# A three-layer graph network on one core: layers one and two multiplied in pairs of states by Strassen's scheme

## What is computed

```
x = layernorm(x + L0(x, src, dst))          # three layers, this is where the change is
x = layernorm(x + L1(x, src, dst, ...))     # one message-passing block, untouched
def L0(x, Ws_self, Ws_neigh, bs, src, dst):
    deg = segment_sum(ones, dst)
    inv_deg = 1 / clip(deg, 1)
    h = x                                   # 3125 x 512
    for l in range(3):
        neigh = segment_sum(h[src], dst) * inv_deg
        h = h @ Ws_self[l] + neigh @ Ws_neigh[l] + bs[l]
        if l != 2: h = relu(h)
    return h
```

## Time and profile before

| | us |
|---|---|
| median of 3 runs (lowest, highest) | 1944.8 (1929.04, 1958.04) |
| span of the profiled execution | 1942.4 |
| TensorE busy in it | 1847.2 (95%) |
| VectorE busy in it | 1175.3 (61%) |
| ScalarE, GpSimd busy in it | 623.7 (32%), 1137.9 (59%) |

### The profile page before, as it was taken

How to read it: one execution, slowest core, us unless ns; L and a number is a source line. 1 busy time by engine, 2 the same in 40 slices (tenths; PEclk the granted TensorE clock), 3 DMA queues, 4 the chain that set the end, 5 groups by cost and what they waited for, 6 DMA issues and landing times.

```text
span 1942.4 us, 23120 instructions
## 1 busy us (share of the span) xinstructions
PE 1847.2 (95%) x7910; PEld 1133.5 (58%) x7910; DVE 1175.3 (61%) x1955; ACT 623.7 (32%) x1432; POOL 1137.9 (59%) x1087
## 2 busy tenths in 40 slices
PE   8999999999999989999999999999997699999987
PEld 4455555554555545555555556666665477777765
DVE  6866778677444433444344436555535489899977
ACT  1566532332000000000000000111115478788875
POOL 4400000364888877888788822777776667677770
PEclk9999999999999989999999999999998799999998
DMA  5365665433555344544444443566644234344340
GB/s 163 123 210 174 222 206 180 128 102 95 142 145 139 105 128 116 145 124 132 108 132 124 121 130 128 197 210 198 209 157 117 71 96 114 105 109 114 110 109 26
DMA packets 239540, 265.35 MB, mean 137 GB/s; under 512 B 130757, under 2 KB 176527, under 8 KB 239420
## 3 DMA queue, kind: packets, MB, share of 16 engines
q1 hardware_dynamic: 204028, 205.79, 34.7%
q0 software_dynamic: 34480, 57.58, 10.9%
q10 hardware_dynamic: 912, 0.46, 0.1%
HBM read 174.44 MB, written 89.27 MB: 136 GB/s over the span
## 4 chain that ended last, share of the span: by engine, by line
PE 70%; DVE 11%; issue 6%; ACT 4%; another core or an unknown queue 3%; POOL 3%; DMA 2%; SPq 0%; DVEq 0%; POOLq 0%; ACTq 0%
PE low L1228 37%; PE mid L1054 23%; PE low L1258 3%; PE top L1085 2%; DVE table L2023 1%; PE mid L1239 1%; ACT table L1491 1%; DVE sort L1831 1%; PE mid L1069 1%; DVE table L2026 1%; POOL sort L900 1%; POOL table L922 1%; DVE table L2040 1%; DVE wbuf L2002 1%
## 5 line engine op out<-in xcount | busy, mean ns | idle before, releaser
L1228 PE MATMUL low<-table,abuf 125*125 125x512 f16 x3750 | 844.0, 382 | 7.3 <-issue 7.2
L1228 PEld LDWEIGHTS low<-table,abuf 125*125 125x125 bf16 x3750 | 508.3, 137 | 315.2 <-issue 43.4
L1054 PE MATMUL mid<-wbuf,h_t 128*125 128x512 f32 x1200 | 556.5, 601 | 5.8 <-DVE st_out L1759 5.1
L917 POOL DMA_INDIRECT by_src<-scat_row,sort x416 | 487.1, 1171 | 126.1 <-issue 120.8
L922 POOL DMA_INDIRECT table<-msg_table,wbuf x270 | 294.3, 1090 | 128.3 <-issue 85.2
L1054 PEld LDWEIGHTS mid<-wbuf,h_t 128*125 128x125 f32 x1200 | 215.4, 189 | 217.3 <-issue 202.5
L1769 DVE SCALAR_TENSOR_TENSOR y<-low,inv_deg,st_in 125x512 f32<-125x512 f32 x75 | 56.1, 749 | 462.1 <-PE low L1228 309.7
L1713 DVE TENSOR_TENSOR abuf<-abuf,row_scale 125x750 bf16<-125x750 bf16 (+6 forms) x156 | 265.9, 1719 | 0.8
L949 POOL DMA_INDIRECT sort<-msg_table,sort x180 | 193.2, 1073 | 92.2 <-issue 54.5
L1258 PE MATMUL low<-table,wbuf 128*125 128x256 f32 x900 | 212.7, 387 | 18.1 <-ACT table L1491 11.2
L900 POOL TENSOR_TENSOR sort<-sort 128x416 f32<-128x416 f32 x26 | 31.9, 1226 | 320.7 <-DVE sort L1831 320.7
(11 more groups left out here) (245 smaller groups left out, 1595.8 us busy)
## 6 DMA issues: line engine op xcount, KB each, us to landing
abuf<-adj SPq DMA_DIRECT2D x75, 781.2 KB
adj<-table SPq DMA_DIRECT2D x25, 781.2 KB, 4.6
states<-st_out SPq DMA_DIRECT2D x75, 256.0 KB
st_in<-states SPq DMA_DIRECT2D x75, 256.0 KB
flips<-y_flip SPq DMA_DIRECT2D x48, 256.0 KB
h_t<-flips SPq DMA_DIRECT2D x192, 64.0 KB
early_rows<-sort POOLq DMA_DIRECT2D x35, 320.0 KB
table<-early_rows SPq DMA_DIRECT2D x24, 448.0 KB
```

The source lines that it names most:

```text
L917: pool.indirect_dma_start(out=by_src, out_offset=bass.IndirectOffsetOnAxis(ap=place_i[:, k * PIECE + j:k * PIECE + j + 1], axis=0), in_=sc ...
L1054: last = pe.matmul(to[0:TN, :], h_t[i % 2][:, k, 0:TN], weights[l % 2][:, a, k, :], start=k == 0, stop=k == KC - 1)
L1228: last = pe.matmul(p_agg[k % 2][0:TN, :], a_tile[k % 3][:, a, :], table[ps % 2][0:TN, a, h, :], start=a == 0 and h == 0, stop=a == TILES - ...
```

## The change

In each of the layers one and two, 22 of the 25 states are taken in pairs (r, q = r + 1). With the columns of a state cut in two halves of 256 and each weight matrix cut likewise, the two states' rows and own parts are four sums of eight *half products* (a half product is two f32 matmuls); the changed kernel forms them from seven half products with Strassen's sums of states and of weights. A pair takes 14 f32 matmuls in place of 16. Both states of a pair are multiplied in one aggregate (k % 25 = 3, 5, ... 23; r = k + 22), and the aggregate before or after it holds none. The states 22, 23 and 24 of a layer stay as they were.

- TensorE: `pair_first(r)` at a = 4 (four half products, in `p_pair`, which are the four banks of `mid`), `pair_second(r)` at a = 16 (three). In `pair_first` the second half product waits for `s_mixed`, that is for VectorE's `mix_states`; `pair_second` waits for `s_own` of r, that is for `unmix_first`.
- VectorE: `mix_states(r)`, four f32 instructions on 128 x 250, right behind `flip` in the pair's step; `unmix_first` (four on 125 x 512) behind the edge sort's first part; then `unmix_rows`, `row_scales` and `row_lo` of r and of q, `unmix_second`, all before the edge sort's second part. Two `own_part` go. `mix_weights` (four instructions on 128 x 1024) runs once a layer, at k = 1 and k = 26.
- ScalarE: `copy_first(r)` copies one PSUM bank to `st_out`; in k under 7 it stands between the first and the second block eviction. Both `row_hi` stand behind the last eviction.
- SyncE: `h_t` has four buffers in place of two; the weights of layer two are loaded at k = 25 in place of k = 2, because the mixed weights of a layer lie where the other layer's are.
- Some tiles of the sort share memory with other things; the masks of the bins wait for `bin_starts` in place of the counts.

```diff
     for a in range(TILES):                              # TensorE, aggregate k
-        for state in made_at(k):
+        for r in pair_begun(k):
+            if a == 4:
+                pair_first(r)
+        for r in pair_ended(k):
+            if a == 16:
+                pair_second(r)
+        for state in singles_at(k):
...
+    def pair_first(r):
+        for i in (r, q):
+            pe.wait_ge(s_fld[flips_to(i) % 2], flips_loaded(flips_to(i)))
+        pe.wait_ge(s_wmix, 1 + l)
+        pe.wait_ge(s_row, r)
+        pe.wait_ge(s_own, r)
+        pair_product(p_pair[0], h_t[q % HT][:, 0:HALF, :], upper).then_inc(s_half, 1)
+        pe.wait_ge(s_mixed, 1 + n + 1)
+        pair_product(p_pair[1], mixed[:, 1, :, :], wm[:, 0, HALF:KC, :]).then_inc(s_half, 1)
+        pair_product(p_pair[2], mixed[:, 0, :, :], wm[:, 0, 0:HALF, :]).then_inc(s_half, 1)
+        pair_product(p_pair[3], h_t[r % HT][:, 0:HALF, :], wm[:, 1, 0:HALF, :]).then_inc(s_ps, 1)
+    def pair_second(r):
+        pe.wait_ge(s_own, r + 1)
+        pair_product(p_pair[3], h_t[r % HT][:, HALF:KC, :], wm[:, 1, HALF:KC, :], False).then_inc(s_pn, 1)
+        pair_product(p_pair[0], h_t[q % HT][:, HALF:KC, :], w[:, 0, HALF:KC, :], False).then_inc(s_pn, 1)
+        pair_product(p_pair[2], mixed[:, 2, :, :], w[:, 1, HALF:KC, :], False).then_inc(s_ps, 1)
...
+    def mix_states(r):                                  # VectorE
+        for i in (r, q):
+            dve.wait_ge(s_fld[flips_to(i) % 2], flips_loaded(flips_to(i)))
+        ch.link(dve.tensor_tensor(s1, upper_r, lower_r, ALU.add))
+        dve.tensor_tensor(upper_r, upper_q, upper_r, ALU.subtract)
+        ch.link(dve.tensor_tensor(s2, s1, upper_q, ALU.subtract))
+        dve.tensor_tensor(s4, lower_q, s2, ALU.subtract).then_inc(s_mixed, 1)
...
         if k and by_dma(i):
             flip(i)
+        for one in pair_begun(k):
+            mix_states(one)
...
         place_bins(bins_first(k))
         if k == 13:
             places_last()
-        for state in made_at(k):
+        for one in pair_begun(k):
+            unmix_first(one)
+        for one in pair_ended(k):
+            unmix_rows(one)
+            for i in (one, one + 1):
+                row_scales(i)
+                row_lo(i)
+            unmix_second(one + 1)
+        if k in (1, TILES + 1):
+            mix_weights(k // TILES + 1)
+        for state in singles_at(k):
```

More of the change, by code:

```diff
@@ L144, in gnn_kernel @@
     y_flip = sb("y_flip", [P, D])
-    h_t = [sb(f"h_t{b}", [P, KC, P]) for b in range(2)]
+    h_t = [sb(f"h_t{b}", [P, KC, P]) for b in range(HT)]
+    mixed = sb("mixed", [P, 3, KC // 2, TN])
+    deg_row = mixed[0:TILES, 0, 0, :]
     row_max = sb("row_max", [P, 1])
@@ L312, in gnn_kernel @@
     p_s = p_mid[:, 3 * D:4 * D]
+    p_pair = [p_mid[:, b * D:(b + 1) * D] for b in range(4)]
     p_b = [p_top[:, 0:D], p_top[:, D:2 * D]]
@@ L517, in made_at, with paired, pair_begun, pair_ended @@
         return [n for n in (i - 1,) if by_dma(n)] + [n for n in (i,) if TILES <= n < AGGS and not by_dma(n)]
+    def paired(i):
+        return TILES <= i < AGGS and i % TILES < PAIRED
+    def pair_begun(k):
+        r = k + PAIRED
+        return [r] if k < 2 * TILES and 3 <= k % TILES <= PAIRED + 1 and k % TILES % 2 else []
+    def pair_ended(k):
+        return pair_begun(k)
+    def pair_ended_last(k):
+        return bool(pair_ended(k)) and first_tile(k + 1)
+    def pair_number(r):
+        l, t = divmod(r, TILES)
+        return (l - 1) * (PAIRED // 2) + t // 2
+    def rows_bank(i):
+        if paired(i):
+            return p_pair[3] if i % TILES % 2 == 0 else p_pair[0]
+        return p_n[i % 2]
+    def singles_at(k):
+        return [i for i in made_at(k) if not paired(i)]
+    def stored_at(k):
+        return pair_begun(k) + [r + 1 for r in pair_ended(k)] + singles_at(k)
     def flips_loaded(n):
@@ L782, in _ @@
                 if not first_tile(k):
-                    for i in made_at(k):
+                    for i in stored_at(k):
                         store_state(i)
@@ L1053, in product @@
                         pe.wait_ge(s_w0[k], 16)
-                    last = pe.matmul(to[0:TN, :], h_t[i % 2][:, k, 0:TN], weights[l % 2][:, a, k, :], start=k == 0, stop=k == KC - 1)
+                    last = pe.matmul(to[0:TN, :], h_t[i % HT][:, k, 0:TN], weights[l % 2][:, a, k, :], start=k == 0, stop=k == KC - 1)
                     if k == KC - 1:
@@ L1058, in product, with pair_product @@
                         between(a * KC + k)
+            def pair_product(to, rows, cols, first=True):
+                for c in range(HALF):
+                    last = pe.matmul(to[0:TN, :], rows[:, c, 0:TN], cols[:, c, :], start=first and c == 0, stop=c == HALF - 1, skip_group_check=True)
+                return last
+            def pair_first(r):
+                q, l, n = r + 1, r // TILES, pair_number(r)
+                upper = weights[l % 2][:, 0, 0:HALF, :]
+                for i in (r, q):
[5 more added lines that the diff above has]
+                pe.wait_ge(s_mixed, 1 + n + 1)
+                wm = weights[(l + 1) % 2]
+                pair_product(p_pair[1], mixed[:, 1, :, :], wm[:, 0, HALF:KC, :]).then_inc(s_half, 1)
+                pair_product(p_pair[2], mixed[:, 0, :, :], wm[:, 0, 0:HALF, :]).then_inc(s_half, 1)
+                pair_product(p_pair[3], h_t[r % HT][:, 0:HALF, :], wm[:, 1, 0:HALF, :]).then_inc(s_ps, 1)
+            def pair_second(r):
+                q, l = r + 1, r // TILES
+                w, wm = weights[l % 2], weights[(l + 1) % 2]
+                pe.wait_ge(s_own, r + 1)
+                pair_product(p_pair[3], h_t[r % HT][:, HALF:KC, :], wm[:, 1, HALF:KC, :], False).then_inc(s_pn, 1)
+                pair_product(p_pair[0], h_t[q % HT][:, HALF:KC, :], w[:, 0, HALF:KC, :], False).then_inc(s_pn, 1)
+                pair_product(p_pair[2], mixed[:, 2, :, :], w[:, 1, HALF:KC, :], False).then_inc(s_ps, 1)
             def message_product(i):
@@ L1068, in message_product @@
                 for k in range(4):
-                    last = pe.matmul(p_n[i % 2][0:TN, k * F:(k + 1) * F], h_t[i % 2][:, k, 0:TN], w_in_sb[:, min(k, 1), :], start=True, stop=True)
+                    last = pe.matmul(p_n[i % 2][0:TN, k * F:(k + 1) * F], h_t[i % HT][:, k, 0:TN], w_in_sb[:, min(k, 1), :], start=True, stop=True)
                 last.then_inc(s_pn, 1)
@@ L1939, in _ @@
                     one_hot_rows(builder_of(TILES + k + 1))
-                if k + 1 < AGGS:
+                if k + 1 < AGGS and not pair_ended_last(k):
                     scale(k + 1, 0)
```

101 lines of the change are left out of this document (75 added, 26 removed).

## The result

The changed kernel takes 2056.3 us (median of 4 runs, 2030.4 to 2067.8) against 1946.4 (4 runs): ratio 1.054, 95% interval 1.045 to 1.064. It is slower by 110 us where +60 was forecast, and lies above the range.

A forecast was written before the change was run, and what follows sets the result against it. TensorE, busy 95%, was taken to bound the kernel, with VectorE as full in aggregates 1 to 13. 71.4 us lost there less 11 gained later gave +60, about 2004 us (+3%), range 1968 to 2034.

The forecast's parts named there:

- the early stage: Aggregates 1 to 13, with six pairs: VectorE's backlog makes TensorE wait for mixing; loss of 71.4 us.
- Walk: Step-by-step timing of aggregates 1 to 13: aggregate 13 ends at 550.3, where it ended at 478.9 before.
- chain: From aggregate 7 on, VectorE and TensorE wait in turn: two steps take 49.5 us, against 37.1 for VectorE now.
- Prices: VectorE's added instructions: mixing about 1.70 us, `mix_weights` 4.9, adds 0.70 each; in all +4.5 us a pair.
- the other sixteen pairs: Pairs at k = 15 to 23 and 28 to 48: VectorE has room, 0.7 us gain a pair, 11 us in all.
- I take 1.0 of waiting in all: Waiting per pair for mix and flips in the sixteen later pairs, leaving 0.7 us of gain each.
- one quiet step: Timeline step where VectorE takes the mean 0.2 us after its aggregate ends; mix then ready at 4.0 us.
- 12.5 us of time for 10 to 12 of way: Later pairs: newer state's flip arrives 10 to 12 us behind the previous aggregate's end, when 12.5 have gone.
- `mix_weights` at k = 26: Mixing of layer two's weights: costs nothing, since it ends a step or more before it is needed.
- The clock falls at every pair: Rival: 1 us waits also cost 3 us of slow clock, sixteen pairs lose 48 us: 2050 us; chance 0.06.
- The smaller loss: Rival: low prices, waits too short for the clock to fall: +24 to +40, 1968 to 1984 us; chance 0.16.
- the gain: Rival: VectorE's mean keeps up in aggregates 3 to 13; 22 pairs give 20 to 25 us, 1920 to 1925; chance 0.08.

The follow-up runs named there:

- Experiments 2: Changed kernel with pairs only in aggregates 3 to 13 of pass 0, all later states multiplied singly: 2013.3 us, ratio 1.039.
- 4: Changed kernel, all pairs, with the three scans ending steps 8 and 10 moved into steps 9 and 11: 2025.2 us, ratio 1.046.
- Experiment 5: Kernel with pairs only from aggregate 15 on, 390 of GpSimd's 416 edge-row scatters left out: aggregates 14 to 49 take 636.0 us; whole time says nothing.
- 3: Kernel with pairs only from aggregate 15 on, first part of a pair at a = 8 in place of 4: 1930.0 us, ratio 0.996.
- 7: Kernel with pairs only from aggregate 15 on, flips issued ahead of the adjacency tile's load in steps before a pair: 1963.6 us, ratio 1.012.
- late pairs: Changed kernel with pairs only from aggregate 15 of pass 0 on and in pass 1, 16 pairs, weights mixed in aggregate 14: 1989.8 us.
- both remedies: Pairs only from aggregate 15 on, parts at a = 10 and 17, flips ahead of the tile's load: 2050.9 us first time, 1927.3 us (ratio 0.992) second.
- experiment 11: Kernel with pairs only from aggregate 15 on, first part at a = 4, second at a = 11 in place of 16: 2083.2 us, 1 run.
- 9: First run of pairs only from aggregate 15 on, parts at a = 10 and 17, flips ahead of the tile's load: 2050.9 us, ratio 1.016, unclear.
- 12: Second run of pairs only from aggregate 15 on, parts at a = 10 and 17, flips ahead of the tile's load: 1927.3 us, ratio 0.992.

## Why the prediction was wrong

**Right: the early stage.** Walk and chain hold: 71.4 us were forecast to aggregate 14, and 552.1 - 478.9 = 73.2 measured; the walk ended the aggregates 3, 7 and 11 at 301.0, 400.2 and 499.3, the trace has 299.3, 397.8 and 499.7. Prices hold: mixing 1.83 (1.70), adds 0.69 and 0.70 (0.70). Two steps are 473.87 - 422.95 = 50.9 by VectorE's means (49.5). Experiments 2 and 4 show the cause. Within the sum, places were exchanged: waits for the mixing are 4.2, 3.8, none, 11.7, 11.3 and 12.8, where 5 to 9 stood, and TensorE waits for flips not at all in 7, where I had 4.4, and only 1.0 to 1.5 in 9, 11 and 13. In aggregates 2, 4 and 6 TensorE stands for the blocks' evictions, 3.5, 8.6 and 6.8 us, where the walk had late scaling in 5 and 6: ScalarE's evictions stand behind its relu, and that behind VectorE's late mean. It is the same lag, seen through another engine.

**Wrong: "the other sixteen pairs".** The term was -11 us and measured +37.9 (waits 26.6, stalls 11.1, clock 26.4, saving 27.5). The step that failed is "I take 1.0 of waiting in all", with nothing beside it for slow clock or for stalls inside the aggregates. The waits are no even 1.0 but 0.2 to 3.4 us, 1.7 on average; the longer ones bring the clock down, and that makes more of the miss than their length does. The 1.0 rests on a mean 0.2 us behind its aggregate, taken from one quiet step. In the pair steps the mean comes late, 3.4 us in the case above, and the flips, which I had at 12.5 us of time for 10 to 12 of way, have no room for that. I had noted how close they are and priced the closeness at 0.4. Experiment 5 shows the rest of the term right in the steps where means are in time; 3 that a later place removes the loss, 7 that an earlier issue removes most of the waits. `mix_weights` at k = 26, put at nothing, costs nothing in the changed kernel (the pair in 28 waits 0.3 us) but does in experiment 5.

**The rivals.** "The clock falls at every pair" came near the time, 2050, with only part of the mechanism, so that its closeness is partly luck: slow clock is 26 us where it had 48. In the second stretch the granted clock fell to 0.50, the level of 1.2 GHz, behind seven of the eight waits of 1.98 to 3.44 us and stayed at 1.00 behind all shorter ones, up to 1.76; the rival had it fall behind 1. The smaller loss and the gain did not come, since VectorE's lag is there. In the late pairs alone, with both remedies, the gain comes: 24.9 us for sixteen, 1.6 a pair.

**Open.** Why the signal is late in nearly every pair step and only in some steps of single states was not found; experiment 11, a single run, speaks against the place of the second part alone. Why stalls come in long sequences of aggregate matmuls was not tried either, and they differ between two traces of the same kernel (24.5 and 8.1 us in 9 and 12).

## What to carry to other kernels

A saving on the busiest engine is worth what its new waits leave: ask of each producer that the new consumer meets in mid-stream how far it trails there, in the crowded stages first. Where a transfer's way and its time differ by less than a few us, price the spread of its start over many steps, not one quiet step; a later place for the consumer cost nothing that could be measured here. Look also at what the change does to the order behind it: work that is put together in one place leaves a long unbroken sequence elsewhere, in which 11 us of stalls came here. And take such a change only in the stages where the producers have room: with late pairs and both remedies the same scheme is 0.8% faster, in all pairs 5.4% slower.

## What the runs showed of the hardware

Under GpSimd's scatters the signal of a finished group of matmuls reached VectorE and SyncE 3.4 us (in experiment 11 8.5 us) behind the last matmul's end, while TensorE went on; and TensorE had stalls of 0.15 to 2.1 us inside aggregates, for which the profile shows no wait. In the kernels before and after, all of these stalls (9 and 25) came behind 40 or more aggregate matmuls in a row. With 390 of 416 scatters left out late signals and stalls were gone, and the 36 aggregates of the kernel before fell from 649.8 to 637.4. By which way the scatters act on TensorE's signals was not tried.
